# Gates' stage: the last gate product ahead of the neighbours' product, a graph finished one slot later

## The reference

```python
# layer 0
h = max(layernorm(x), 0)
c = relu(bn(conv1x1(h.T)));  x_conv = relu(bn(conv17(c)) + h.T).T
s = h @ w_se.T + b_se
A = exp(-dist(s)) * adj
x_nmp = A @ relu(h @ w_msg.T + b_msg)
gi = [x_conv, x_nmp] @ w_ih.T + b_ih;  gh = h @ w_hh.T + b_hh
r, z = sigmoid(gi_r + gh_r), sigmoid(gi_z + gh_z)
n = tanh(gi_n + r * gh_n)
x1 = x + (1 - z) * n + z * h
# layer 1
h2 = max(layernorm(x1), 0)
out = x1 + relu(h2 @ w1[:256] + (adj @ h2) @ w1[256:] + bias)
```

## Time and profile before

| | us |
|---|---|
| median of 3 runs | 1869.83 |
| lowest and highest of them | 1867.81, 1880.15 |
| profiled execution | 1870.98 |
| its span, first to last instruction | 1868.8 |
| granted TensorE clock, mean over the span | 0.992 |

### The profile page before, as it was taken

The page is one execution under the profiler, slowest core; times in us unless marked ns, Lnnn a source line. Parts: engine busy times, 40 slices in busy tenths (PEclk is TensorE's granted clock), DMA queues, the critical chain, the costliest instruction groups (busy, mean ns, idle before and its releaser), DMA issues.

```text
span 1868.8 us, 36896 instructions
## 1 busy us (share of the span) xinstructions
PE 1768.8 (95%) x12477; PEld 1167.3 (62%) x12478; DVE 1495.5 (80%) x3322; ACT 875.8 (47%) x1617; POOL 439.2 (24%) x616
## 2 busy tenths in 40 slices
PE   3768999999998999999999999999999999999996
PEld 1456777764445666666666666666666666666664
DVE  4899999962346888888888888888888888888886
ACT  3675555553344444444444444444444444444442
POOL 4511111101012222222222222222222232222221
PEclk9899999999999999999999999999999999999999
DMA  6298887767732322322322322322322322322320
GB/s 201 98 331 261 303 295 270 265 224 250 253 132 94 104 76 81 102 78 80 101 79 80 100 80 79 100 81 78 99 83 76 99 84 75 100 85 74 101 86 17
DMA packets 175187, 245.56 MB, mean 131 GB/s; under 512 B 14781, under 2 KB 111028, under 8 KB 174635
## 3 DMA queue, kind: packets, MB, share of 16 engines
q1 hardware_dynamic: 175128, 244.81, 39.9%
HBM read 154.57 MB, written 90.18 MB: 131 GB/s over the span
## 4 chain that ended last, share of the span: by engine, by line
PE 40%; DVE 21%; ACT 5%; issue 3%; DVEq 0%; POOL 0%; POOLq 0%
PE ps_rz L1551 18%; PE ps_l L1551 13%; PE ps_n L1551 7%; ACT big L1696 3%; ACT big L1591 3%; DVE big L1687 2%; DVE big L1586 2%; DVE big L1621 2%; DVE big L1643 2%; DVE big L1595 2%; DVE big L1578 2%; DVE big L1730 2%; DVE big L1704 2%; PE ps_d L1765 2%; DVE big L1734 2%
## 5 line engine op out<-in xcount | busy, mean ns | idle before, releaser
L1551 PE MATMUL ps_rz<-big 128*128 128x512 f16 x2304 | 560.6, 379 | 13.0 <-DVE big L1643 10.7
L1551 PEld LDWEIGHTS ps_rz<-big 128*128 128x128 f16 x2304 | 220.0, 98 | 224.0 <-DVE big L1643 20.0
L1551 PE MATMUL ps_n<-big 128*128 128x256 f16 x2304 | 314.2, 273 | 0.0
L1551 PEld LDWEIGHTS ps_n<-big 128*128 128x128 f16 x2304 | 225.3, 98 | 94.5
L1551 PE MATMUL ps_l<-big 128*128 128x512 f16 (+1 forms) x1536 | 271.9, 327 | 2.9 <-DVE big L1800 1.5
L1264 PE MATMUL m_ps<-big 128*128 128x512 f16 (+1 forms) x1152 | 268.3, 375 | 3.0 <-DVE big L1029 2.2
L1721 POOL TENSOR_TENSOR big<-big 128x256 f32<-128x256 f32 x128 | 97.5, 762 | 666.9 <-ACT big L1714 666.9
L1696 ACT ACTIVATE big<-big,w_scale 128x512 f32<-128x512 f32 x128 | 92.0, 719 | 283.3 <-DVE big L1687 283.3
L1551 PEld LDWEIGHTS ps_l<-big 128*128 128x128 f16 x1536 | 149.9, 98 | 90.9 <-DVE big L1800 2.0
L1551 PE MATMUL ps_b<-big 128*128 128x256 f16 x1536 | 188.6, 272 | 1.5 <-DVE big L1621 1.5
L1264 PEld LDWEIGHTS m_ps<-big 128*128 128x128 f16 x1152 | 111.8, 98 | 105.1 <-issue 2.2
(11 more groups left out here) (242 smaller groups left out, 2892.7 us busy)
## 6 DMA issues: line engine op xcount, KB each, us to landing
spectra<-ysb SPq DMA_DIRECT2D x96, 256.0 KB, 2.4
big<-spectra SPq DMA_DIRECT2D x64, 384.0 KB, 3.5
xin<-in_x SPq DMA_DIRECT2D x64, 256.0 KB, 4.0
x_normed<-front SPq DMA_DIRECT2D x64, 256.0 KB, 4.3
h_turned<-front SPq DMA_DIRECT2D x64, 256.0 KB, 3.9
big<-h_turned SPq DMA_DIRECT2D x64, 256.0 KB, 3.2
big<-in_adj SPq DMA_DIRECT2D x64, 256.0 KB, 3.6
big<-in_x SPq DMA_DIRECT2D x64, 256.0 KB, 2.8
```

The lines of the kernel that those rows point to most:

```text
L1551: last = pe.matmul(dest, stationary(dl), moving(wl), start=start and n == 0, stop=stop and n == 2, **kw)
```

## The change

- On PE, `gates_second` of row 1 stands ahead of `neighbours` instead of behind it.
- On DVE, `gate_sums` of row 1 moves from the head of the next slot to the end of the graph's own slot.
- `finish` is cut in two: `out_row` (L1817's operation, once for each row) and the rest (L1821's). Both run one slot later, for graph t-2 instead of t-1, and no longer at the slot's end: `out_row` of row 0 stands ahead of `weighted_low`, `out_row` of row 1 behind `adj_split_low`, the rest behind `h2_split_low`.
- `adj_split_low` moves from ahead of `weighted_low` to behind `norm2`. With that, `norm2`, which normalises x1, comes directly behind `weighted_low` as before, and `weighted_low` directly behind `out_row` of row 0.
- SP stores graph t-2 instead of t-1. Each engine's `slot` gets an argument for this, and there is one slot more at the end, in which only DVE and SP have work.

```diff
--- before.py
+++ after.py
@@ -1808,30 +1808,32 @@
                                  lambda s: u_s[:, s, m, :], False, m == H - 1, skip_group_check=True)
                 last.then_inc(S["out_done"], 1)
 
+        def out_row(dve, t, p, i):
+            ready(dve, "out_done", t, i + 1, H)
+            dve.scalar_tensor_tensor(out=out_sum[:, i, :], in0=ps_l[i][:, 0:D], scalar=w["scale"][:, 11:12],
+                                     in1=w["bias_out"][:, :], op0=ALU.mult,
+                                     op1=ALU.add).then_inc(S["out_added"], 1)
+
         def finish(dve, t, p):
             if not (isinstance(t, int) and t < 2):
 
                 dve.wait_ge(stored[p], (t - p) * 8)
             for i in range(H):
-                ready(dve, "out_done", t, i + 1, H)
-                dve.scalar_tensor_tensor(out=out_sum[:, i, :], in0=ps_l[i][:, 0:D], scalar=w["scale"][:, 11:12],
-                                         in1=w["bias_out"][:, :], op0=ALU.mult,
-                                         op1=ALU.add).then_inc(S["out_added"], 1)
                 ready(dve, "out_added", t, i + 1, H)
                 dve.scalar_tensor_tensor(out=out_sb[:, p, i, :], in0=out_sum[:, i, :], scalar=0.0, in1=x1[:, p, i, :],
                                          op0=ALU.max, op1=ALU.add).then_inc(S["out_ready"], 1)
 
-
         def slots(engine, slot):
 
-            slot(0, 0, False, True, True)
-            slot(1, 1, True, True, True)
+            slot(0, 0, False, False, True, True)
+            slot(1, 1, False, True, True, True)
             with engine.Fori(1, (graphs - 2) // 2) as j:
                 for p in range(2):
-                    slot(j * 2 + p, p, True, True, True)
-            slot(graphs - 2, 0, True, True, True)
-            slot(graphs - 1, 1, True, True, False)
-            slot(graphs, 0, True, False, False)
+                    slot(j * 2 + p, p, True, True, True, True)
+            slot(graphs - 2, 0, True, True, True, True)
+            slot(graphs - 1, 1, True, True, True, False)
+            slot(graphs, 0, True, True, False, False)
+            slot(graphs + 1, 1, True, False, False, False)
 
         with nc.Block() as block:
             @block.sync
@@ -1839,13 +1841,13 @@
                 for i in range(3):
                     sp.wait_ge(early.y_stored[i], 16 * (2 * HALF_UNITS * graphs // GROUP // 3))
 
-                def slot(t, p, prev, cur, nxt):
+                def slot(t, p, old, prev, cur, nxt):
                     if nxt:
                         load_rows(sp, t + 1, 1 - p)
                         load_h(sp, t + 1, 1 - p)
                         load_x(sp, t + 1, 1 - p)
-                    if prev:
-                        store(sp, t - 1, 1 - p)
+                    if old:
+                        store(sp, t - 2, p)
 
                 slots(sp, slot)
                 for i in range(2):
@@ -1905,9 +1907,8 @@
             def _(dve):
                 conv_split_low(dve, 0, 0)
 
-                def slot(t, p, prev, cur, nxt):
+                def slot(t, p, old, prev, cur, nxt):
                     if prev:
-                        gate_sums(dve, t - 1, 1 - p, 1)
                         gate_new(dve, t - 1, 1 - p, 1)
                     if cur:
                         attention(dve, t, p)
@@ -1917,15 +1918,22 @@
                     if prev:
                         x1_rows(dve, t - 1, 1 - p, 1)
                         x1_stats(dve, t - 1, 1 - p, 1)
+                    if old:
+                        out_row(dve, t - 2, p, 0)
                     if cur:
-                        adj_split_low(dve, t, p)
                         weighted_low(dve, t, p)
                     if prev:
                         norm2(dve, t - 1, 1 - p)
                     if cur:
+                        adj_split_low(dve, t, p)
+                    if old:
+                        out_row(dve, t - 2, p, 1)
+                    if cur:
                         gate_sums(dve, t, p, 0)
                     if prev:
                         h2_split_low(dve, t - 1, 1 - p)
+                    if old:
+                        finish(dve, t - 2, p)
                     if cur:
                         gate_new(dve, t, p, 0)
                         x1_rows(dve, t, p, 0)
@@ -1934,8 +1942,8 @@
                         passed_low(dve, t - 1, 1 - p)
                     if nxt:
                         conv_split_low(dve, t + 1, 1 - p)
-                    if prev:
-                        finish(dve, t - 1, 1 - p)
+                    if cur:
+                        gate_sums(dve, t, p, 1)
 
                 slots(dve, slot)
 
@@ -1965,10 +1973,10 @@
                     if cur:
                         first_conv_rz(pe, t, p, 1)
                         first_conv_n(pe, t, p, 1)
+                    if cur:
+                        gates_second(pe, t, p, 1)
                     if prev:
                         neighbours(pe, t - 1, 1 - p)
-                    if cur:
-                        gates_second(pe, t, p, 1)
 
                 slots(pe, slot)
 

```

## The result

The changed kernel takes 1859.88 us in the median of five runs (1858.36 to 1861.13), the kernel before 1868.76 in five runs beside them (1867.81 to 1880.15). The ratio is 0.9944 with a 95% interval from 0.9917 to 0.9971: 0.6% faster, so within the 1% band. The forecast was 1858.4.

What follows compares the result with a forecast made beforehand. PE, busy 95% of the span, was taken as the bound, pausing for DVE's L1643. 10.1 + 1.3 = 11.4 us off the profiled 1870.98 gave 1859.6, as a median 1858.4 (forecast 1853 to 1864; range 1852 to 1873).

Steps and rivals of the forecast that it cites:

- The wait for L1643: Gates' stage: with L1578 out of the way, PE's gate product starts 0.16 us earlier in 63 slots, 10.1 us.
- the gate product's move in the middle of the stage: Mid-stage, it frees DVE earlier ahead of L1621 and x1's rows, where PE didn't pause: counted 0.
- The tail: Program's end: graph 63's chain up to the last transposes starts 1.31 us earlier, counted once, 1.3 us (0 to 1.3).
- The finish at no cost: DVE: finish's four instructions one slot later fit in gaps or leave enough margin, so they cost 0.
- The delay of gate_new: DVE: two L1821 in front make gate_new start 0.74 us later; counted 0.
- The 1.4 us to spare: L1800 on DVE, though delayed, ends 1.4 us before PE's neighbours' product needs it.
- norm2 directly behind L1643: DVE: norm2 follows L1643 at once, from 14.01 to 14.75, as x1 is ready 0.72 us earlier.
- The floor of 0.92: PE's least time from inverse transform to gate product, 0.92 us or a little more; upper bound of gain 0.25 a slot.
- Rival A: Behind norm2, adj's low half loses the shared ports to POOL's conv_add: 1.1 us a slot lost, about 1938; chance 0.05.
- Rival B: Row 0's gate_sums on DVE come late without blocking, PE stalls 0.27 us a slot: 1875; chance 0.09.
- Rival C: L1643's wait only changes its name, or L1643 comes no earlier; tail or nothing left: 1868 to 1870; chance 0.13.
- Rival D: PE gains more than the wait, reaching its floor or recovering hidden lost time: under 1851; chance 0.03.

Runs made afterwards that it cites:

- Experiment 1: The kernel before with only adj's low half moved behind norm2; ratio to before 0.9952, 19.829 us a slot.
- experiment 3: The changed kernel with adj's low half back ahead of the weighted messages' low half (L1643); ratio to before 0.9945, 19.844 us a slot.
- experiment 8: The kernel of Experiment 7 plus twenty unused matmuls on PE ahead of the last transposes; ratio to before 0.9870, 19.670 us a slot.
- experiment 4: The changed kernel with row 1's gate product back behind the neighbours' product, its gate sums at the next slot's head; ratio to before 1.0026.
- experiment 9: The kernel of experiment 4 with the two last instructions of finish behind gate_new of row 0; ratio to before 0.9957, 19.827 us a slot.
- Experiment 5: The changed kernel plus one unused DVE instruction of 384 elements behind the second out_row; ratio to before 0.9930, 19.825 us a slot.
- experiment 6: The kernel of Experiment 5 with the second out_row and the extra instruction ahead of adj's low half; ratio to before 1.0105, 20.325 us a slot.
- Experiment 2: The kernel before with row 1's gate product ahead of the neighbours', its gate sums at slot's end ahead of the old finish; ratio to before 1.0155.
- Experiment 7: The changed kernel with row 1's first six products into ps_rz between inverse transform and row 0's gate product; ratio to before 0.9891.

## Why the prediction was right, point by point

- **The wait for L1643: 0.16 a slot.** Measured 0.162, and L1643 starts 0.03 behind ACT, the gate product 1.01 behind the inverse, both as worked out. Experiment 1 shows that the step named, L1578 out of the way, is enough for all of it. What I counted as 0, the gate product's move in the middle of the stage, does it too, once the finish stands one slot later (experiment 3); as a term of the sum 0 was right, since the second cure has nothing left to cure.
- **The tail: 1.3.** The transposes came 1.31 us sooner, but only about 0.6 us of it stayed in the two profiles: from the last L1643 to the span's end 33.2 us before and 32.6 after. The first-layer product grew by 0.84 us at the lower granted clock, which I didn't look at. That product took anything from 4.13 to 5.30 us over the kernels of this study but the eighth, whichever order they had, so its growth isn't shown to come from the change; experiment 8 shows that the clock sets its length. Over more profiles the term is about 0.9: the stretch from the last L1643 to the end has a mean of 33.5 us with the old order on PE (33.2, 34.1, 33.4, 33.4 in before and experiments 1, 4, 9) and of 32.6 with the gate product first (32.6, 32.1, 33.0, 32.7 in the changed kernel and experiments 3, 5, 6). Experiment 2, whose old finish holds DVE up, is left out. So this term was mis-sized: 1.3 was too much, in the right direction.
- **The finish at no cost.** Right for the changed kernel, and the cover that I named is the real one: experiment 4 takes it away (the neighbours' product back in its place) and the finish costs 0.26 us a slot. The delay of gate_new, predicted as 0.74, is 0.67. The 1.4 us to spare that I gave L1800 (measured: it ends at 1019.49, the product starts at 1021.21) was the whole difference between gain and loss.
- **norm2 directly behind L1643.** It came so, but not for my reason. x1's statistics (L1742) stand ahead of L1578 in the kernel before, so x1 could not come earlier by L1578's 0.72. What L1578 held up was POOL's L1746, 0.61 us in the earlier trace rows and 0.20 in the changed kernel (at 1008.72) and in experiment 1, where norm2 also follows L1643 directly; in the changed kernel x1 is earlier besides, by the gate product's move.
- **The floor of 0.92.** Wrong: I took it from graph 0's slot, where PE also follows L1643 directly, by 0.06. Experiment 7 gives 0.85. It was only an upper bound of the gain, so it did no harm there, but it hid 0.16 us a slot that were still to be had.
- **Rival A.** The exclusion is real and goes by order of start (experiment 6); it didn't decide, since adj's low half started 0.73 us ahead of conv_add (0.55 by my sum). Nor did POOL's row get longer, as I had forecast: conv_add takes 1.16 in both, since adj's low half was over. The price, a stall of 1.25 us a slot before the gain comes off, was probably too high. Experiment 6 stalls for 0.50, but has the out_row ahead of adj's low half; with its 0.4 us behind, as in the rival, some 0.9 is my estimate.
- **Rival B.** Not so: DVE came to the sum of ps_rz 0.06 us late (1.56 us behind the gate product's start instead of 1.50), where my sum had 0.29 and this rival 0.81. Experiment 5 shows room for one more instruction of 0.6 us.
- **Rivals C and D** did not occur, though D was right that PE had more to gain: experiment 7 took it.

The sum over the profiled execution was 11.4 and the spans differ by 11.1. That they agree so closely is in part luck, since 0.3 of the 11.1 lies ahead of the first L1643 and has nothing to do with the change; the stage gave 10.2, and the tail 0.6 in these two profiles. In the timed medians it is 8.9 us, with an interval of the ratio that reaches from 5 to 16 us.

## What to carry to other kernels

An instruction that nobody waits for yet doesn't belong between a chain's two links: look at what stands ahead of the late link on its engine, and move that, before moving anything larger. When a piece has to leave its place, put it where its engine waits for another one (behind gate_new here), not at the nearest point where its input is ready. And when the profile lists no more waits on the bounding engine, compare the distances between starts with the same group elsewhere: a pause of 0.16 us a slot stood in no list of waits.

## What the runs showed of the hardware

- The clock of PE in the tail was worth more here than unused matmuls in idle time cost. After 5.25 us of idle time, the transposes and 1.42 us more of it, the stretch with the first-layer product was granted 0.61 of 2.4 GHz, so it ran mostly at the lower level of 1.2 GHz, and twelve matmuls took 5.04 us; with 4.48 us of unused matmuls in the first of these idle times, the stretch was granted 1.00, and they took 2.76.
- A scalar_tensor_tensor with both tensors in SBUF and a tensor_tensor on POOL hold each other up: the first takes 0.75 us alone and 1.51 when POOL had started 0.20 ahead, with its last 0.55 behind POOL's end; the second takes 1.16 alone and 1.49 when it started 0.47 ahead of the other's end. The Trainium skill, SBUF — State Buffer, "Who interferes with whom", states the rule (whichever is issued first keeps the shared ports); experiment 6 agrees with it in the order.
- The same first stage took up to 12 us more or less from one profiled execution to another (559.2 to 571.6 us to the stage's start), more than the whole effect studied here. That is why experiment 1 has a span of 1866.5 us and yet the changed kernel's slot: its first L1643 comes 7.2 us later.
